# Rows of V for six batches from two three-column products and a DMA, and three Gram products moved from steps 7, 9, 11 to steps 1, 3, 5

## The reference

```
k1, k2, v1, v2 = x + x @ W.T + b        for each of the four weights
S1 = k1^T v1 / n,  S2 = k2^T v2 / n      per head, 8 x 8
v1m, v2m = mean of v1, v2 over the rows
out = (q @ S1) * v2m * g1 + sum(S1*S2) * g2 + (q @ S2) * v1m * g3 + (q @ (S1*S2)) * g4
```

## Time and profile before

| | us |
|---|---|
| median of 3 runs (lowest to highest) | 211.31 (209.78 to 213.27) |
| the profiled execution | 209.8 |
| its span, first to last instruction | 208.1 |
| PE busy (share of the span) | 191.7 (92%) |
| DVE busy | 161.8 (78%) |
| POOL busy | 136.3 (66%) |
| ACT busy | 127.8 (61%) |

### The profile page before, as it was taken

How to read it: one execution, slowest core, us unless ns; L and a number is a source line. 1 busy time by engine, 2 the same in 40 slices (tenths; PEclk the granted TensorE clock), 3 DMA queues, 4 the chain that set the end, 5 groups by cost and what they waited for, 6 DMA issues and landing times.

```text
span 208.1 us, 4250 instructions
## 1 busy us (share of the span) xinstructions
PE 191.7 (92%) x1377; PEld 176.2 (85%) x1377; DVE 161.8 (78%) x478; ACT 127.8 (61%) x383; POOL 136.3 (66%) x177
## 2 busy tenths in 40 slices
PE   6949999999999999999999999999999999999930
PEld 6838998998898979897989999998989899988620
DVE  0265854988879887989698787977798869896895
ACT  0342439364659575966596667758585659785571
POOL 8904651474697758984898379756897389876130
PEclk9999999999999999999999999999999999999995
DMA  5999700000000100110010101010011001011012
GB/s 154 243 191 289 185 0 5 2 0 5 0 15 35 54 2 0 55 50 0 0 54 4 48 3 50 2 54 0 2 50 55 0 3 50 0 52 54 2 50 101
DMA packets 12116, 9.98 MB, mean 48 GB/s; under 512 B 727, under 2 KB 9950, under 8 KB 12094
## 3 DMA queue, kind: packets, MB, share of 16 engines
q1 hardware_dynamic: 11056, 8.52, 13.2%
q0 software_dynamic: 448, 0.92, 2.5%
q10 hardware_dynamic: 590, 0.26, 0.6%
HBM read 5.51 MB, written 4.19 MB: 47 GB/s over the span
## 4 chain that ended last, share of the span: by engine, by line
PE 73%; DVE 12%; issue 4%; DMA 4%; POOL 4%; ACT 2%; DVEq 0%; POOLq 0%; ACTq 0%
PE down_ps L904 25%; PE up_ps L904 20%; PE prep_ps L904 11%; PE z_ps L904 10%; DMA late_rows<-in_L_ffn_b 4%; PE turn_ps L1031 3%; PE turn_ps L1002 2%; DVE y2n L705 2%; DVE st L700 2%; DVE down_ps L749 2%; DVE E_sb L769 1%; DVE x1T_lo L840 1%; DVE y2n L870 1%; DVE V_sb L775 1%; ACT res L580 1%
## 5 line engine op out<-in xcount | busy, mean ns | idle before, releaser
L904 PE MATMUL down_ps<-w_sb,hT 128*128 128x128 f32 x496 | 61.0, 277 | 0.1
L904 PEld LDWEIGHTS down_ps<-w_sb,hT 128*128 128x128 f32 x496 | 58.4, 192 | 1.2 <-DVE y2n L705 0.4
L597 ACT ACTIVATE hT<-up_ps,cols 128x512 f32<-128x512 f32 x64 | 41.7, 681 | 4.4 <-PE up_ps L904 4.2
L580 ACT ACTIVATE res<-y,nb,rstd 128x128 f32<-128x128 f32 x60 | 24.7, 483 | 7.5 <-POOL nb L471 7.5
L509 POOL TENSOR_TENSOR x1b<-x,b_rows 128x512 f32<-128x512 f32 x16 | 20.6, 1286 | 10.1 <-DVE x L705 10.1
L904 PE MATMUL up_ps<-x1T_hi,w_hi 128*128 128x512 f32 x64 | 26.0, 406 | 0.5 <-ACT hT L597 0.5
L904 PE MATMUL up_ps<-x1T_lo,w_hi 128*128 128x512 f32 x64 | 25.4, 398 | 0.0
L904 PE MATMUL up_ps<-x1T_hi,w_lo 128*128 128x512 f32 x64 | 25.3, 396 | 0.0
L558 ACT ACTIVATE z_sq<-z_ps 128x128 f32<-128x128 f32 x64 | 16.8, 270 | 11.4 <-PE z_ps L904 11.4
L498 POOL TENSOR_TENSOR xu<-X,u_rows 128x512 f32<-128x512 f32 x16 | 19.0, 1187 | 6.0 <-DVE u_rows L696 6.0
L705 DVE TENSOR_SCALAR x<-z_ps,st,rstd 128x128 f32<-128x128 f32 x64 | 21.9, 404 | 0.1
(11 more groups left out here) (151 smaller groups left out, 416.5 us busy)
## 6 DMA issues: line engine op xcount, KB each, us to landing
X<-in_L_attn_x SPq DMA_DIRECT2D x8, 512.0 KB, 9.9
out<-res SPq DMA_DIRECT2D x15, 256.0 KB, 2.0
w_sb<-in_L_ffn_w POOLq DMA_DIRECT2D x2, 256.0 KB, 9.8
out<-res SPq DMA_DIRECT2D x2, 128.0 KB, 1.9
w_raw<-in_L_attn_Wv ACTq DMA_DIRECT2D x2, 64.0 KB, 2.8
w_raw<-in_L_attn_Wk SPq DMA_DIRECT2D x2, 64.0 KB, 4.0
bv_rows<-in_L_attn_bv ACTq DMA_DIRECT2D x2, 64.0 KB, 6.0
g_row<-in_L_attn_g ACTq DMA_DIRECT2D x4, 0.1 KB
```

What stands on the lines that cost most here:

```text
L580: last = act.activation(res[buf][:, t, :], y3[buf][:, t, :], ACT.Identity, scale=rstd4[:, t:t + 1], bias=nb4[:, t:t + 1])
L597: act.activation(hT[:, k, :], up_ps[k % len(up_ps)][:, :], ACT.Relu, bias=cols[:, 5 + k:6 + k]).then_inc(relu_out, 1)
L904: return pe.matmul(o, lhsT, rhs, start=start, stop=stop)
```

## The change

Batches 0 and 1 stay as they are, with EV_out split into E_out and V_out. For batches 2 to 7:

- `gram_av` runs only the first of its two products, and DVE makes only E_sb.
- Two new products, `v_rows(0)` for batches 2, 3, 4 at the end of step 0 and `v_rows(1)` for batches 5, 6, 7 in step 7 after the first `up`, take three columns of G_sb as weights and A_v as the moving side. They give three rows of 256 numbers in prep_ps, on partitions 0, 1 and 2. DVE adds the bias into V_rows (in steps 1 and 7, after y2n).
- SP issues, for each of the two sets, three DMAs (`place_v`), one for each batch: the source is one row of V_rows (1 KB, on one partition, read 128 times), the destination 128 partitions of V_all. The first set stands in SP's queue ahead of the store of group 0, the second ahead of the store of group 5. All three must have landed before `prepare` on POOL and `s_out` on DVE pass (V_landed, 48).
- The Gram products of batches 5, 6, 7 are in steps 1, 3, 5, since `v_rows(1)` needs all three. `gram_av` of step 2, 4, 6 waits for that step's Gram result to be copied out.

The diff, cut to its core:

```diff
+            def wait_v(eng, b):
+                if b >= 2:
+                    eng.wait_ge(V_landed[(b - 2) // VSET], 16 * VSET)
         def prepare(eng, b):
-            eng.wait_ge(EV_out, b + 1)
+            eng.wait_ge(V_out, min(b, 1) + 1)
+            wait_v(eng, b)
...
-                self.gram = n % 2 == 1 and has(3) and self.seq(3) >= EARLY
+                self.gram = EARLY + n // 2 if n in (1, 3, 5) else None
+                self.v_set = {0: 0, 7: 1}.get(n)
+                self.v_rest = {1: 0, 7: 1}.get(n)
...
+            def place_v(v):
+                sp.wait_ge(rows_out, v + 1)
+                for i in range(VSET):
+                    sp.dma_start(V_all[:, v * VSET + i, :, :].rearrange("p j c -> p (j c)"),
+                                 V_rows[i:i + 1, v, :, :].rearrange("p j c -> p (j c)").unsqueeze(1).to_broadcast([1, 128, 256])).then_inc(V_landed[v], 16)
             def store(b):
                 for g in range(1 if b == BATCHES - 1 else SEQ_GROUPS):
+                    if (b, g) in ((0, 0), (2, 1)):
+                        place_v(b // 2)
...
+                if st.v_rest is not None:
+                    dve.wait_ge(rows_done, st.v_rest + 1)
+                    dve.tensor_tensor(V_rows[:, st.v_rest, :, :]..., prep_ps[0:VSET, 0:256],
+                                      nbv_rows[0:VSET, :, :]..., ALU.add).then_inc(rows_out, 1)
...
             def gram_av(b):
+                if b >= 2:
+                    wait(pe, G_out, min(BATCHES, b + 4))
+                    if b == 5:
+                        pe.wait_ge(rows_out, 2)
+                    mm(prep_ps[:, 0:256], G_sb[:, b, 0:C], A_kv[:, 0:2, :]...).then_inc(ev_done, 1)
+                    return
...
+            def v_rows(v):
+                b = 2 + v * VSET
+                pe.wait_ge(G_out, b + VSET)
+                pe.wait_ge(PQfix_out, 2 if v == 0 else 5)
+                mm(prep_ps[0:VSET, 0:256], G_sb[:, b:b + VSET, C], A_kv[:, 1:3, :]...).then_inc(rows_done, 1)
...
             def ak_e(b):
-                wait(pe, EV_out, b + 1)
+                wait(pe, E_out, b + 1)
...
+                if st.v_set == 1:
+                    v_rows(1)
```

More of the change, by code:

```diff
@@ L43 @@
 EARLY = 5
+VSET = 3
 def build(nc, x, Wq, bq, Wk1, bk1, Wk2, bk2, Wv1, bv1, Wv2, bv2, g1, g2, g3, g4, ln_g, ln_b, Wo, bo,
@@ L106, in build @@
         V_sb = sb("V_sb", [128, 2, 128])
+        V_rows = sb("V_rows", [VSET, 2, 2, 128])
+        V_all = sb("V_all", [128, 2 * VSET, 2, 128])
         S_sb = sb("S_sb", [128, 2, 128])
@@ L215, in build @@
         relu_out = sem("relu_out")
-        EV_out = sem("EV_out")
+        E_out = sem("E_out")
+        V_out = sem("V_out")
+        rows_done = sem("rows_done")
+        rows_out = sem("rows_out")
+        V_landed = [sem("V_landed0"), sem("V_landed1")]
         S_out = sem("S_out")
@@ L306, in ev_bank, with v_of @@
             return up_ps[2] if b == 1 else prep_ps
+        def v_of(b):
+            return V_sb[:, :, :] if b < 2 else V_all[:, b - 2, :, :]
+        def wait_v(eng, b):
+            if b >= 2:
+                eng.wait_ge(V_landed[(b - 2) // VSET], 16 * VSET)
         def rows(t, n=TILES):
@@ L323, in s_out @@
         def s_out(dve, b):
-            wait(dve, EV_out, b + 1)
+            wait(dve, V_out, min(b, 1) + 1)
             wait(dve, s_done, b + 1)
+            wait_v(dve, b)
             for j in range(2):
-                last = dve.scalar_tensor_tensor(out=S_sb[:, j, :], in0=V_sb[:, 1 - j, :],
+                last = dve.scalar_tensor_tensor(out=S_sb[:, j, :], in0=v_of(b)[:, 1 - j, :],
                                                 scalar=cols[:, j:j + 1],
@@ L339, in prepare @@
             k = b * 4
-            eng.tensor_tensor(gv[:, :, :], V_sb[:, :, :], gmask[:, 0:2, :], ALU.mult).then_inc(m_step, 1)
+            eng.tensor_tensor(gv[:, :, :], v_of(b), gmask[:, 0:2, :], ALU.mult).then_inc(m_step, 1)
             if b == 0:
@@ L649, in body @@
                     gram_out(4)
-                if st.gram:
-                    gram_out(st.seq(3))
+                if st.gram is not None:
+                    gram_out(st.gram)
             run_steps(body)
@@ L771, in body @@
                                              scalar=G_sb[:, b, C:C + 1], in1=ev_bank(b)[:, 0:256],
-                                             op0=ALU.mult, op1=ALU.add)
+                                             op0=ALU.mult, op1=ALU.add).then_inc(E_out, 1)
                     if b == 0:
                         dve.wait_ge(nbv_ready, 1)
-                    dve.tensor_tensor(V_sb[:, :, :].rearrange("p j c -> p (j c)"), ev_bank(b)[:, 256:512],
-                                      nbv_rows[:, :, :].rearrange("p j c -> p (j c)"), ALU.add).then_inc(EV_out, 1)
+                    if b < 2:
+                        dve.tensor_tensor(V_sb[:, :, :].rearrange("p j c -> p (j c)"), ev_bank(b)[:, 256:512],
+                                          nbv_rows[:, :, :].rearrange("p j c -> p (j c)"), ALU.add).then_inc(V_out, 1)
+                if st.v_rest is not None:
+                    dve.wait_ge(rows_done, st.v_rest + 1)
+                    dve.tensor_tensor(V_rows[:, st.v_rest, :, :].rearrange("p j c -> p (j c)"), prep_ps[0:VSET, 0:256],
+                                      nbv_rows[0:VSET, :, :].rearrange("p j c -> p (j c)"), ALU.add).then_inc(rows_out, 1)
                 if st.n == -2:
@@ L945, in gram @@
                 if b >= EARLY:
-                    pe.wait_ge(PQfix_out, b)
+                    pe.wait_ge(PQfix_out, b - EARLY + 2)
+                    pe.wait_ge(rows_out, 1)
                 for t in tiles:
@@ L967, in gram_av @@
             def gram_av(b):
+                if b >= 2:
+                    wait(pe, G_out, min(BATCHES, b + 4))
+                    if b == 5:
+                        pe.wait_ge(rows_out, 2)
+                    mm(prep_ps[:, 0:256], G_sb[:, b, 0:C], A_kv[:, 0:2, :].rearrange("p j c -> p (j c)")).then_inc(ev_done, 1)
+                    return
                 wait(pe, G_out, b + 1)
@@ L972, in gram_av @@
                    A_kv[:, 1:3, :].rearrange("p j c -> p (j c)")).then_inc(ev_done, 1)
+            def v_rows(v):
+                b = 2 + v * VSET
+                pe.wait_ge(G_out, b + VSET)
+                pe.wait_ge(PQfix_out, 2 if v == 0 else 5)
+                mm(prep_ps[0:VSET, 0:256], G_sb[:, b:b + VSET, C], A_kv[:, 1:3, :].rearrange("p j c -> p (j c)")).then_inc(rows_done, 1)
             def attention_matrix(b):
@@ L990, in ak_e @@
             def ak_e(b):
-                wait(pe, EV_out, b + 1)
+                wait(pe, E_out, b + 1)
+                if b < 2:
+                    wait(pe, V_out, b + 1)
                 for j in range(2):
@@ L1098, in body @@
                     last.then_inc(down_done, 1)
-                if st.gram:
-                    gram(st.seq(3), range(0, SEQ_TILES // 2))
+                if st.gram is not None:
+                    gram(st.gram, range(0, SEQ_TILES // 2))
                     turn_x1(n + 1, True)
-                    gram(st.seq(3), range(SEQ_TILES // 2, SEQ_TILES))
+                    gram(st.gram, range(SEQ_TILES // 2, SEQ_TILES))
                 elif st.nxt and st.nxt2:
                     turn_x1(n + 1, True)
+                if st.v_set == 0:
+                    v_rows(0)
             run_steps(body)
```

## The result

The changed kernel takes 223.31 us as a median of four runs (222.65 to 224.8), the kernel before 211.25 (209.78 to 213.27). The ratio is 1.0644, with a 95% interval of 1.0587 to 1.0701: slower by 6.4%, which is 13.6 us of 211.25; the two medians by themselves are 12.1 us apart, and in the two traces the stretch from the first to the last `product` grew by 13.8. I had forecast slower, 219, with a range of 208 to 223. The direction was right and the wait came where it was forecast; the size was 4 us short and the median lies just above the range, as a part of the loss was missing from the sum.

A forecast was written before the change was run, and what follows sets the result against it. PE was taken to bound pairs with a Gram product, DVE's chain the others. Removals -2.31, new products +0.86 and DMA stalls +10.1 us gave +8.7, so 219 us as a median, range 208 to 223.

The forecast's parts named there:

- The two kinds of pair and what V is worth in each: Step pairs with a Gram product are PE-bound, gaining 0.43 us each; those without are DVE-bound, gaining 0.34 each; together 2.31.
- Moving the Gram products: Gram products with their ACT copies go to steps 1, 3, 5; costed at nothing, perhaps a few tenths.
- The DMAs, the step of which I was least sure: Each set's three DMAs into V_all land 16 us after issue, the engines sharing about 26 GB/s from one partition.
- the price in the Trainium skill: A DMA costs about 2.0 us plus bytes at 436 GB/s, an estimated 2.9 us for a set.
- The stalls: PE waits before the attention matrix in steps 2 and 8 for late DMAs: 4.5 and 5.6 us.
- The two new products: Three-column products on PE in steps 0 and 7, 0.43 us each, cost 0.86.
- fewer weight columns could only make them cheaper: For the three-column products on PE: 0.43 us each by the row of `gram_av`, with narrower weights costing no more.
- The clock: PE's granted clock behind the stalls in steps 2 and 8: the forecast's sum gave it no cost.
- rival C: The stall in step 8 lowers PE's clock to 1.2 GHz, costing 3 us more, 222 in all; chance 0.08.

The follow-up runs named there:

- e2: The kernel before with only the Gram products of batches 5, 6, 7 moved to steps 1, 3, 5; ratio to the kernel before 1.0014.
- e3: The changed kernel with the same six DMAs read from 128 partitions of a constant buffer instead of one partition 128 times; ratio to the kernel before 1.0003.
- e5: The kernel before with ten extra 128 KB DMAs, alone and in pairs; pairs from partitions 0+1 and 0+32 took 11.8 us, 0+4 and 0+64 9.6 to 10.0.
- e4: The changed kernel with 38 unused products on PE where it stalls in steps 2 and 8; 218.39 us, ratio to the kernel before 1.0423.
- e1: The changed kernel with a semaphore for each DMA, so steps 2 and 8 wait for the first alone; ratios to the kernel before 0.9965 and 0.9935.
- e7: e1 with the weights of the three-column products widened to 96 columns, copied by POOL; 208.01 us, ratio to the kernel before 0.9933.
- e9: e1, but steps 2 and 8 wait for the first two DMAs of their set; ratio to the kernel before 1.0007.

## Why the prediction was off

*The two kinds of pair and what V is worth in each: right.* Between the first and the last `product` the kernel before takes 161.58 us, the changed one 175.37, 13.79 more. The removal gives 0.43 and 0.45 in pairs 3+4 and 5+6, and 0.33 in 9+10 and 11+12, against 0.43 and 0.34 forecast. *Moving the Gram products: right,* e2. *The DMAs, the step of which I was least sure: right in size,* 16 us taken, 16.1 and 16.3 measured, at 28 GB/s. The number is better than its ground: it was picked between bounds, as the share of one engine in 410 GB/s, for 16 engines that want the same partition. e3 shows that the source sets it; that it is a single partition is what e5 speaks against. One reading beside it was loose: the prediction says that rows 8 agree with the price in the Trainium skill ("DMA: Bandwidth & Descriptors", Anatomy of one DMA), but that price is given for DMAs that GpSimd issues, and for 256 KB it comes to an estimated 2.6 us where rows 8 have 2.0. *The stalls: right.* Without the clock's part they are 15.81 - 11.41 = 4.40 in step 2 and 17.80 - 12.28 = 5.52 in step 8 (e4 less e1), against 4.5 and 5.6.

*The two new products: too cheap,* 0.86 forecast, 1.44 measured, 0.6 us. The sentence that fewer weight columns could only make them cheaper is wrong: with three they cost 0.3 us more each than with 96 (e7).

*The clock: this is the step that failed.* The forecast's sum priced each stall of PE at its length and the work behind it at full clock; the term for the clock stood at nothing. I had it as rival C with a chance of 0.08, for step 8 alone, at 3 us, and left it out of the forecast and of the range's upper end. Both stalls lowered it, and it cost 2.21 and 2.47, 4.68 us together. I had read the earlier trace rows as if a stall had to be about as long as the idle time ahead of that fall, 4.0 us (PE's end at 199.3, the fall at 203.3). Those rows show only one fall. In step 2 the clock fell 2.1 us after PE's last instruction and in step 8 3.8 after it, while a stall of 0.9 in e9 left it full; what length of stall is enough these runs don't say. With a stall of 4 to 6 us forecast twice, the clock belonged in the forecast's own sum.

With +1.44 for the two products, +9.92 for the stalls and +4.68 for the clock, 13.79 leaves -2.25 for V's work. That term is a remainder, so the sum proves nothing by itself; the gains of the pairs named above are what supports it.

| term, us | forecast | measured |
|---|---|---|
| V's product and V_sb removed | -2.31 | -2.25 (remainder) |
| two three-column products | 0.86 | 1.44 |
| Gram products moved | 0 | 0 (e2) |
| stalls in steps 2 and 8 | 10.1 | 9.92 |
| clock behind them | 0 | 4.68 |
| sum | 8.7 | 13.79 |

## What to carry to other kernels

A DMA's source counts as much as its destination: one row of one partition, repeated 128 times, came at 28 GB/s here, where each of the same DMAs from 128 partitions landed in 2 us. Price it by the source, expect whatever is queued beside it to land late, and give each piece a semaphore of its own: here the first piece was all that was needed at once, and that alone took the whole loss away. Where a forecast has PE idle for some microseconds in mid-kernel, add the clock to the price of the idle time. Where two engines take turns in setting the pace, find out in each stretch whose work it is before pricing a removal.

## What the runs showed of the hardware

- 128 KB from one partition to 128 landed 6.3 to 6.9 us after its issue, from 128 partitions 2.0 to 2.1; three in a row out of partitions 0, 1 and 2 ran at 28 GB/s, the last landing 15.0 us after its issue.
- DMAs in two queues from partitions 0 and 1, or 0 and 32, took 11.8 us from first issue to last landing; from 0 and 4, or 0 and 64, 9.6 to 10.0. A store of 256 KB issued between the two landed after 9.5 us in the first case and after 5.0 to 5.2 in the second, against 2.0 alone; behind the second set of the changed kernel one landed after 11.7.
- A product with three weight columns took 0.71 to 0.73 us of PE's time, with the same 256 columns moving and 96 weight columns 0.41 to 0.43.
- PE's granted clock fell to half, 1.2 GHz, at 61.9 with PE idle since 59.9 and at 137.0 with PE idle since 133.3, and came back 4.8 and 5.4 us after PE's work had begun again. That cost 2.2 and 2.5 us. 38 products without use in the two holes kept it at 2.4 GHz.
